# SyncE's loads in another order, and a front end that takes four batches through first

## What is computed

```python
# block 1: 16 heads of 8, one set of keys and values for all 8 batches
q = relu(queries @ Wq_w.T + Wq_b); k = relu(keys @ Wk_w.T + Wk_b); v = relu(values @ Wv_w.T + Wv_b)
attn = softmax(einsum('bhsd,bhtd->bhst', qh, kh) / sqrt(8), axis=-1)
a = einsum('bhst,bhtd->bhsd', attn, vh)
return a.transpose(0, 1, 3, 2).reshape(q.shape) + queries
# block 2: attention over the 8 batches (4 heads of 32), then 8 experts
y1 = ln(x + mha(x)) * g1 + b1
y2 = ln(y1 + moe(y1)) * g2 + b2     # moe: top-1, capacity 512, gate * ((x @ w1 + b1) @ w2 + b2)
```

## Time and profile before

| what | value |
|---|---|
| median of 3 runs | 668.88 us (664.58 to 671.4) |
| profiled execution, its own time | 670.79 us |
| its span in the profile | 669.0 us |
| PE, DVE, ACT, POOL busy | 532.2, 539.4, 429.6, 229.0 us |
| mean granted TensorE clock | 0.892 of full |
| DMA | 28.92 MB in 31285 packets |
| loop (first columns' scores to the last `attended` copy) | 72.2 to 402.2 us |
| back end | from 402.3 us |

### The profile page before, as it was taken

The page is one execution under the profiler, slowest core; times in us unless marked ns, Lnnn a source line. Parts: engine busy times, 40 slices in busy tenths (PEclk is TensorE's granted clock), DMA queues, the critical chain, the costliest instruction groups (busy, mean ns, idle before and its releaser), DMA issues.

```text
span 669.0 us, 9878 instructions
## 1 busy us (share of the span) xinstructions
PE 532.2 (80%) x3439; PEld 212.6 (32%) x3439; DVE 539.4 (81%) x867; ACT 429.6 (64%) x914; POOL 229.0 (34%) x360
## 2 busy tenths in 40 slices
PE   2884799999999998999999988476587685998710
PEld 1550122222222222222222215355467542443300
DVE  4969699999999998999999800988838156899996
ACT  2550489998898888988889885134344404566554
POOL 7001000000034440354403650662344401676761
PEclk9995599999999999999999999688687775999955
DMA  9832010111111111201221002000000000000112
GB/s 243 255 136 106 14 37 23 40 33 46 54 60 30 34 53 47 65 26 32 59 57 49 8 9 62 15 1 1 0 1 1 1 1 0 0 1 0 32 31 63
DMA packets 31285, 28.92 MB, mean 43 GB/s; under 512 B 6132, under 2 KB 23676, under 8 KB 31236
## 3 DMA queue, kind: packets, MB, share of 16 engines
q1 hardware_dynamic: 29204, 27.31, 13.8%
q10 hardware_dynamic: 2032, 0.98, 0.6%
HBM read 19.23 MB, written 8.65 MB: 42 GB/s over the span
## 4 chain that ended last, share of the span: by engine, by line
PE 38%; DVE 27%; POOL 15%; ACT 8%; issue 8%; DMA 3%; SPq 1%; ACTq 0%; DVEq 0%; POOLq 0%
PE ps L1267 11%; PE ps L1262 8%; DVE row_max L1436 8%; PE ps L1235 4%; PE ps L593 3%; DVE space L872 2%; DVE st L241 2%; POOL space L382 2%; POOL space L384 2%; POOL smallp L379 2%; ACT attended L1384 1%; DMA space<-max_turned 1%; PE ps L578 1%; DVE space L863 1%; DVE space L264 1%
## 5 line engine op out<-in xcount | busy, mean ns | idle before, releaser
L1436 DVE TENSOR_REDUCE row_max<-ps 128x2 f32<-128x1024 f32 x256 | 299.7, 1219 | 20.2 <-PE ps L1235 17.3
L1368 ACT ACTIVATE space<-ps 128x512 f32<-128x512 f32 x512 | 271.9, 605 | 45.0 <-PE ps L1262 44.5
L1262 PE MATMUL ps<-space 51*128 51x512 bf16 x512 | 159.5, 388 | 9.6 <-DMA space<-max_turned 5.8
L1267 PE MATMUL ps<-space 128*32 128x512 f32 x1024 | 138.1, 612 | 3.0 <-ACT space L1368 0.7
L1235 PE MATMUL ps<-space 48*128 48x512 bf16 x512 | 128.8, 401 | 14.2 <-DVE row_max L1436 12.5
L1137 POOL CAST max_parts<-row_max 128x16 bf16<-128x16 f32 x32 | 6.3, 197 | 269.9 <-DVE row_max L1436 269.9
L1262 PEld LDWEIGHTS ps<-space 51*128 51x128 bf16 x512 | 41.2, 94 | 170.9 <-ACT space L1368 149.1
L593 PE MATMUL ps<-W,space 128*128 128x512 f32 x128 | 72.0, 646 | 0.0
L428 POOL TENSOR_TENSOR space<-PC,same_row 128x512 f32<-128x512 f32 x32 | 32.8, 1057 | 62.9 <-DVE PC L768 62.9
L710 ACT ACTIVATE space<-ps,weight 128x128 f32<-128x128 f32 x128 | 34.3, 383 | 21.2 <-PE ps L593 9.5
L1235 PEld LDWEIGHTS ps<-space 48*128 48x128 bf16 x512 | 26.6, 94 | 54.9 <-DVE row_max L1436 49.1
(11 more groups left out here) (192 smaller groups left out, 701.0 us busy)
## 6 DMA issues: line engine op xcount, KB each, us to landing
q_parts_dram<-space SPq DMA_DIRECT2D x2, 1536.0 KB, 5.5
space<-q_parts_dram SPq DMA_DIRECT2D x64, 48.0 KB
attended_dram<-attended SPq DMA_DIRECT2D x128, 18.0 KB
X<-in_L_attn_queries SPq DMA_DIRECT2D x8, 256.0 KB, 7.7
space<-in_L_ffn_w SPq DMA_DIRECT2D x2, 1024.0 KB, 5.9
space<-q_parts_dram SPq DMA_DIRECT2D x64, 32.0 KB
space<-attended_dram SPq DMA_DIRECT2D x16, 128.0 KB, 2.4
space<-inverses_dram SPq DMA_DIRECT2D x16, 128.0 KB
```

The lines of the kernel that those rows point to most:

```text
L1262: pe.matmul(ps[:, col_bank(v), :], k_rows[rows_a, kappa // 4 % 2, tc * P:(tc + 1) * P], q_stack[rows_a, kappa % 4, b * S:(b + 1) * S], sta ...
L1267: mm = pe.matmul(ps[32 * m:32 * m + 32, PV, :], v_heads[:, tc, PAIR * (kappa // 4) + m % PAIR, :], probs[:, tc % 2, m, :], start=(tc == 0) ...
L1368: act.activation(probs[:, tc % 2, m, :], ps[:, col_bank(v), :], ACT.Exp, scale=1.0 / math.sqrt(DH)).then_inc(s_pr, 1)
L1436: dve.tensor_reduce(row_max[:, par].rearrange("p (a c) -> p a c", a=PAIR)[:, :, item], ring(n), AX.X, MAX).then_inc(s_free, 1)
```

## The change

Four things are changed together.

1. SyncE's slot: `store_attended` and `load_shift` come first, then `load_stack` and `load_keys`, then the group's loads. `load_attended` is cut in two: the denominators (`load_denominators`, slot c = 1, at its end) and the rest (slot c = 2, at its end, with `store_inverses`). `load_inverses` stands at the head of slot c = 3. `dve_invert` moves from slot c = 1, tc = 2, to slot c = 2, tc = 1.
2. The normalisations of the four front units: units are taken in pairs, both variances first, and POOL's power (variance to the -1/2) replaces ScalarE's root and VectorE's reciprocal.
3. Batches 0 to 3 go through the whole front end first. Units 2 and 3 are loaded after weights, keys and values have landed, normalised after the first four splits, turned and projected batch by batch between the row scores of slot 0 (banks 6 and 7), and split after the eight reductions of slot 0. `fold_weights(1)` moves behind that, with slot 1's row scores between its experts.
4. `k_dram` has another layout and is written by three transfers, which repeat their source, in place of six; the encoder's weights have a semaphore of their own (`s_win`) and are turned later; the second expert weights and the small rows (`load_rest`) are loaded after the first two stacks.

The core of the diff:

```diff
+        def raise_to_minus_half(pool, k, small):
+            pool.wait_ge(s_var, k + 1)
+            pool.tensor_tensor(small[:, 3, :], small[:, 2, :], neg_half[:], ALU.pow).then_inc(s_sd, 1)
+        q_bank = lambda b: b if b < QB else 6 + b % 2
...
+            load_unit(0)
+            load_unit(1)
...
+            sp.wait_ge(s_w, 16 * 3)
+            sp.wait_ge(s_kv, 32)
+            load_unit(2)
+            load_unit(3)
...
-            for r, (_, part) in enumerate(PRODUCTS):
-                sp.dma_start(k_dram[:, r * DH:(r + 1) * DH, :].rearrange("h d t -> h d t"),
-                             k_parts[:, part, :]).then_inc(s_kst, 16)
+            for part, first, times in ((0, 0, 3), (1, 3, 2), (2, 5, 1)):
+                sp.dma_start(k_dram.rearrange("h d r t -> (h d) r t")[:, first:first + times, :],
+                             k_parts[:, part:part + 1, :].broadcast_to([P, times, S])).then_inc(s_kst, 16)
...
+            sp.wait_ge(s_kst, 16 * PARTS)
+            sp.wait_ge(s_const, 5)
+            load_keys(0)
             store_q(0)
-            sp.wait_ge(s_kst, 16 * len(PRODUCTS))
-            sp.wait_ge(s_const, 6)
-            load_keys(0)
             sp.wait_ge(s_qst[0], 16)
             load_stack(0)
             load_stack(1)
+            load_weights(1)
+            load_rest()
+            sp.wait_ge(s_pr, 1)
+            load_shift(0)
             store_q(1)
             sp.wait_ge(s_qst[1], 16)
             load_stack(2)
...
             def slot(kappa):
+                g, c = kappa // 8, kappa % 8
+                if g and c == 3:
+                    load_inverses(g - 1)
+                if kappa:
+                    sp.wait_ge(s_pve, kappa)
+                    store_attended(kappa - 1)
+                if kappa + 1 < NQ:
+                    sp.wait_ge(s_pr, turn_item(kappa + 1) + 1)
+                    load_shift(kappa + 1)
                 if kappa + 3 < NQ:
                     if kappa:
...
                     if (kappa + 3) % 4 == 0:
                         load_keys((kappa + 3) // 4)
-                if kappa:
-                    sp.wait_ge(s_pve, kappa)
-                    store_attended(kappa - 1)
-                if kappa + 1 < NQ:
-                    sp.wait_ge(s_pr, turn_item(kappa + 1) + 1)
-                    load_shift(kappa + 1)
+                if g and c == 1:
+                    await_attended(g - 1)
+                    load_denominators(g - 1)
+                if g and c == 2:
+                    load_attended(g - 1)
+                    store_inverses(g - 1)
...
@@ TensorE
+            pe.wait_ge(s_Wc, 1)
+            turn_batch(QB)
             pe.wait_ge(s_kl[0], 32)
             pe.wait_ge(s_ql[0], 96)
+            pe.wait_ge(s_qe, QB)
+            score_rows(0, 0, 0)
+            score_rows(1, 0, 1)
+            for b in range(QB, B):
+                project_batch(b)
+                if b + 1 < B:
+                    turn_batch(b + 1)
+                    for item in (2 * (b - QB) + 2, 2 * (b - QB) + 3):
+                        score_rows(item, 0, item)
+            turn_max(0)
             pe.wait_ge(s_qe, B)
...
+            fold_weights(pe, 1, rows_of_second_slot)
+            pe.wait_ge(s_Wc, 2)
+            pe.wait_ge(s_csum, 1)
...
@@ VectorE
+            norm_units(0)
...
+            for b in range(QB):
+                split_q(b)
+            norm_units(2)
...
             for item in range(8):
                 reduce_rows(item, 0, item)
+            for b in range(QB, B):
+                split_q(b)
+            for item in range(8):
+                reduce_rows(8 + item, 1, item)
             dve.wait_ge(s_bw, 2)
...
-                    if g and c == 1 and tc == 2:
+                    if g and c == 2 and tc == 1:
                         dve_invert(dve, g - 1)
```

More of the change, by code:

```diff
@@ L299, in turn_b1, with fold_weights @@
             mm.then_inc(s_b1t, 1)
-        def fold_weights(pe, r):
+        def fold_weights(pe, r, between=lambda j: None):
             pe.wait_ge(s_w12[r], 32)
@@ L965, in _, with load_unit @@
         def _(sp):
-            for u, unit in enumerate(UNITS):
-                for g, b in (unit[0], unit[QB]):
+            def load_unit(u):
+                for g, b in (UNITS[u][0], UNITS[u][QB]):
                     sp.dma_start(X[:, g, b:b + QB], x_tok[g][:, b:b + QB]).then_inc(s_x[u], 16)
+            load_unit(0)
+            load_unit(1)
             for j, row in enumerate((bq, bk, bv)):
@@ L1032, in store_attended, with await_attended, load_denominators, load_attended @@
                     sp.dma_start(dst, attended[32 * m:32 * m + DH + 1, kappa % 2, :]).then_inc(s_ast[kappa % 2], 16)
-            def load_attended(g):
+            def await_attended(g):
                 for par in range(2):
                     sp.wait_ge(s_ast[par], 64 * 4 * (g + 1))
+            def load_denominators(g):
+                for h in range(NH // G):
+                    den = a_dram[:, g * (NH // G) + h:g * (NH // G) + h + 1, DH:DH + 1, :]
+                    sp.dma_start(den_sb[32 * h:32 * h + 32], den.rearrange("b h o (j f) -> (h o j) b f", f=D)).then_inc(s_dl, 16)
+            def load_attended(g):
                 for h in range(NH // G):
@@ L1100, in _ @@
             store_attended(NQ - 1)
+            await_attended(G - 1)
+            load_denominators(G - 1)
             load_attended(G - 1)
@@ L1183, in _ @@
             pe.wait_ge(s_const, 4)
-            pe.wait_ge(s_w, 16 * 5)
-            for j in range(7):
-                mm = pe.transpose(ps[:, 4 + j // 4, (j % 4) * P:(j % 4 + 1) * P], w_in[:, j, :], ident[:])
+            pe.wait_ge(s_w, 16 * 3)
+            for j in range(3):
+                mm = pe.transpose(ps[:, 4, j * P:(j + 1) * P], w_in[:, j, :], ident[:])
             mm.then_inc(s_wt, 1)
@@ L1362, in copy_turned, with copy_batch @@
                 act.copy(max_turned[:, kappa % 2, :], src).then_inc(s_pr, 1)
+            def copy_batch(b):
+                act.wait_ge(s_xt, 2 if b < QB else b - 1)
+                act.copy(featT[:, b], ps[:, q_bank(b), :]).then_inc(s_xtc, 1)
+            for b in range(QB):
+                copy_batch(b)
+                if b:
+                    project_q(act, b - 1)
+            project_q(act, QB - 1)
+            act.wait_ge(s_wt, 2)
+            act.copy(wT[:, 3:7].rearrange("p j f -> p (j f)"), ps[:, 5, :]).then_inc(s_wtc, 1)
+            copy_weights(act, 0)
+            copy_folded(act, 0)
+            copy_batch(QB)
+            for b in range(QB, B):
+                if b + 1 < B:
+                    copy_batch(b + 1)
+                project_q(act, b)
+            copy_turned(0)
+            copy_weights(act, 1)
+            copy_folded(act, 1)
+            act.wait_ge(s_bin, 16 * 3)
             def exps(kappa, tc):
@@ L1389, in _, with at, norm_units @@
             ch = Chain(dve, s_dc)
-            def norm_unit(u):
-                dve.wait_ge(s_x[u], 32)
-                at = lambda t: lambda j: t[:, UNITS[u][j][0], UNITS[u][j][1], :]
-                norm(dve, ch, u, at(X), at(XN)).then_inc(s_xn, 1)
-            norm_unit(0)
-            norm_unit(1)
+            def at(t, u):
+                return lambda j: t[:, UNITS[u][j][0], UNITS[u][j][1], :]
+            def norm_units(first):
+                both = ((first, st6, small), (first + 1, st6p, smallp))
+                for u, stats, scale in both:
+                    dve.wait_ge(s_x[u], 32)
+                    norm_variance(dve, ch, at(X, u), stats, scale)
+                for u, stats, scale in both:
+                    dve.wait_ge(s_sd, u + 1)
+                    norm_apply(dve, at(X, u), at(XN, u), scale).then_inc(s_xn, 1)
+            norm_units(0)
             dve.wait_ge(s_kpe, 1)
@@ L1444, in _ @@
                               ADD).then_inc(s_csum, 1)
-            for item in range(8):
-                reduce_rows(8 + item, 1, item)
             def slot(kappa, between):
```

128 lines of the change are left out of this document (48 added, 80 removed).

## The result

| | before | after |
|---|---|---|
| median | 667.14 us (4 runs) | 725.58 us (4 runs, 722.82 to 729.41) |
| ratio | | 1.086, 95% interval 1.081 to 1.091 |
| span of the profiled execution | 669.0 us | 722.2 us |
| first `attended` copy | 87.92 us | 88.54 us |
| last `attended` copy | 401.64 us | 457.10 us |

What follows compares the result with a forecast made beforehand. VectorE was taken to set the loop's pace at 9.94 us a slot. Loop +9.9 (keys +5.6, chain +8.4, saved -4.1) and front end -7.0 gave 668.9 + 2.9, about 672 us; range 658 to 682.

Steps and rivals of the forecast that it cites:

- the keys: Seven slots where load_keys follows the stack: 1.45 us late, less 0.63 forgiven, 0.8 each, +5.6 us (4.9 to 8.4).
- the inverse chain: Slots 10 to 12 and their like, three times: inversion 0.4, late shift 0.8, late stack 1.6 us; +8.4 (6 to 10).
- the front end: Work before the loop: first columns at 66.2 us instead of 72.20, slot 0 1.0 shorter; -7.0 us (-4 to -10).
- The steady slots: Ordinary loop slots: stack lands 0.58 us late but is hidden, costing 0 (0 to 0.1 for about 20 slots).
- free until 0.63 late: Steady slots: a stack up to 0.63 us late costs nothing, from 0.23 of ready rows plus VectorE's 0.40 idle.
- flight: Landing time after a transfer's issue: taken as 1.95 us for the stack, 1.8 to 2.1 for the keys.
- forgiveness: Lateness taken as free in a slot: 0.63 us for stack or keys, 0.4 for a late shift.
- Rival (b): Steady slots late too: landings of 2.2 to 2.4 us, 0.3 in 20 slots, +6; 680 to 683 us; chance 0.18.
- Saved in the loop: Late shifts of slot 9 and its two like go, 1.2 us each, something for slot 1; -4.1 (3.0 to 5.6).
- rival of the selects beside the splits: Front end: POOL's selects slow VectorE's splits, gain 5 instead of 7 us; within a 0.15 rival of 2 or less.

Runs made afterwards that it cites:

- e11: Kernel before with keys' loads first, then store_attended and the shift, then the stack, so that only the stack comes later; 693.87 us, ratio 1.038.
- e5: Kernel after with twelve more unread products on TensorE ahead of the wait in each of the seven key slots; 713.45 us, ratio 1.068.
- e2: Kernel after with SyncE's old slot and the old place of dve_invert, denominators still loaded first; 672.72 us, ratio 1.006.
- e8: Kernel after with SyncE's old slot, old place of dve_invert and old k_dram layout, denominators still loaded first; 669.45 us, ratio 1.003.
- e10: Kernel before with the denominators' four loads ahead of the other four in load_attended; 669.75 us, ratio 1.001.
- e12: Kernel after with old SyncE slot, dve_invert place and k_dram layout, POOL's memsets ahead of its first powers, selects behind all four; 667.57 us, ratio 0.997.
- e1: Kernel before with SyncE's new slot order and the new place of dve_invert alone; 716.3 us, ratio 1.072.

## Why the prediction was wrong

The two profiles differ by 53.2 us where 2.9 were forecast. Of the 50 us between, the keys have 22.7 (28.3 more than before, forecast 5.6), the inverse chain 15.7 (24.1, forecast 8.4), the front end 7.6, and the other slots 6.5 (2.4 more, where 4.1 less was forecast); the back end took 2.3 off.

**The steady slots: "free until 0.63 late", 0 to 0.1 each.** This step failed first. Its lateness was near (0.58 forecast; 0.57 to 0.96 in e11, 0.76 in the mean), but by luck, from two errors against each other: a flight of 2.3 to 2.7 us for 1.95, and a transfer that starts 8.0 us behind the slot's first rows and not 8.6. The forgiveness was wrong. I added 0.23 us that the rows lie ready and 0.40 us that VectorE idles one step later, as if both were free. The first held: e11's slots forgave 0.19. VectorE's 0.40 is time in which it waits for TensorE; when TensorE is late, the wait grows. With the rest at full price e11 lost 0.57 a slot in its slots 2 to 8, and 9.9 us in all its slots but four; 12.7 more of its +25 us are in the slots 10, 18, 26 and 29, where the stack's waits are 1.3 to 2.7 us. Rival (b) had the steady slots late too, through longer landings, but kept the forgiveness and priced them at 0.3 us in 20 slots. In the kernel after these slots show only 6.5 us, because a long slot gives SyncE its slack back (behind slots 2, 6 and 22 the next one is at 9.94).

**The keys: 7 x 0.8 = 5.6, measured 29.4.** Place and direction were right, the size and one term were not. The lateness was 1.45 less 0.63; the waits are 2.92 us in slot 2 and 2.16 to 2.30 in the others, from a pair of issues of 1.54 us instead of 0.77 (the bound that I named, up to 0.70 us an issue, and did not take) and a flight of 2.56 to 2.75 instead of 1.8 to 2.1. With almost nothing forgiven that is 2.4 us a slot by e5. And a term that wasn't in the sum: 12.6 us of half clock behind the stalls, 1.8 a slot in the mean. The clock was weighed in the front end only.

**The inverse chain: 3 x 2.8 = 8.4, measured 24.5.** The waits stand where they were forecast, at the shift of slot 12 and the stack behind it, and are 2.67 and 2.32 us instead of 1.3 and 2.2 late. The forecast then took some 0.5 and 0.6 us off. The first of these was mis-read from slot 9 before the change, whose shift I had put 1.6 us late; TensorE waited 1.28 for it, and the slot was 1.24 longer, so a late shift was forgiven nothing:

```profile
176.26 0.39 PE L1262 MATMUL ps<-space 51*128 51x512 bf16 x2 [1.28 <-DMA space<-max_turned]
```

The six waits make 14.1 of the 24.5 us. The rest goes with granted clocks of 0.66 to 0.94, a term at nothing in the sum, but no run shows how much of it is the clock.

**Saved in the loop: -4.1.** The slots 9, 17 and 25 went from 11.18, 11.78, 10.65 to 10.69, 10.73, 10.90: 1.3 us in sum. The late shifts did go: TensorE waits for none in these slots. What stands in their place is the late stack, with waits of 0.94, 0.98 and 1.15 us, which the forecast had as free. In the old slot order these slots answer to the keys' issue cost (e2 against e8) and not to the order of the denominators (e10).

**The front end: -7.0, measured +0.6.** The splits ended at 30.8 and not 26.1. Three things were missed: the second unit's load, for which VectorE waited 1.13 us; POOL's memsets beside VectorE's applies (2.7 us); and TensorE's queue, where keys and values stand ahead of the transposes (e12: no earlier than 17.4). The rival of the selects beside the splits was the wrong pair: the subtractions took at most 0.78 us for 0.68; the applies were hit, and by writes. The section that I had cited for the splits, "Who interferes with whom" of "SBUF — State Buffer" in the Trainium skill, also states that `tensor_scalar` can enter a two-port mode, and that in such a mode whichever of VectorE and GpSimd issues first holds the shared ports and fully blocks the other. I had not held it against the applies. With 3.71 and 5.28 us beside memsets and 2.13 without, this trace agrees for memsets, but not for POOL's power, beside which they took 2.13; that the applies ran in such a mode no run shows. Then q took 6.0 us to store for 5.5, and the eight reductions of slot 0, forecast at 9.1 us, took 11.1 (43.5 to 54.6), since TensorE had gone to half clock (0.50 from 42 to 47 us) and interleaved scores with projections at that speed. The second eight began at 61.65 for 53.9, and the columns were at 71.34 for 66.2. Slot 0 did not shorten: 17.2 us to its copy, where 14.7 was forecast.

**Chances.** Slower by over 1% had 0.33, and the top of the range, 682, was rival (b). The four prices that were low (flight, issue, forgiveness, chain) hang, as I read it, on one thing, SyncE's queue having no slack, and so came together; I had added them as if they were independent.

## What to carry to other kernels

In a loop whose pace-setting engine waits for a second one even for 0.4 us a turn, that wait is no reserve: count a late operand of the second engine at nearly full price (here all but 0.19 us). A DMA queue in program order is a schedule: before a load is moved ahead, add up every issue between the moved one and the next operand that is wanted, with the new layout's cost per issue. Look at the granted clock behind every stall of TensorE of some 2 us and price that as well: here 16.8 us of lateness cost 29.4.

## What the runs showed of the hardware

- From the start of the issue of a stack's last transfer to the time at which TensorE went on it took 2.3 to 2.7 us (e11's slots 2 to 8, slot 2 of the kernel after); the shift's flight took 1.95 in the earlier trace rows.
- Seven stalls of 2.2 to 2.9 us in a loop where TensorE was otherwise over 90% busy: behind five of them a part of the slot was at 1.2 GHz, behind two the clock stayed at 1.00. Together they cost 12.6 us beside their lateness; filled with products that nobody reads they cost none of it. The stalls of 0.57 to 0.96 us in e11's slots 2 to 8 left the clock at 1.00.
- SyncE issues one load in 0.41 us and in 0.75 us, by the shape of its source in DRAM (two dimensions or three; medians of e1 and of the kernel after, and 0.38 against 0.76 in e8 and e2).
- POOL's memsets, which read no operand, slowed VectorE's `tensor_scalar` on f32 while they ran: sixteen of them ended 2.7 us later than without (19.1 against 16.3), though they began 0.4 us sooner. POOL's power of 128x8 took 1.64 to 1.75 us.
- The best kernel of the study keeps the old slot and layout and has the new front end with POOL's memsets behind its powers: 667.57 us, ratio 0.997 (0.994 to 1.000), a gain at the edge of what can be measured.
